# Other order tables for the last phase of a fused attention: its back half, the routing beside it, and the products of a constant

## The reference, cut to what matters

```python
G = jnp.cumsum(g, axis=-1)
logits = S * scale + (G[..., :, None] - G[..., None, :])
logits = jnp.where(tri, logits, -1e+30)
P = jax.nn.softmax(logits, axis=-1)
o = jnp.einsum('bhij,bhjd->bhid', P, v)
...
topv, topi = jax.lax.top_k(logits, TOP_K)
w = jax.nn.softmax(topv, axis=-1)
hidden = jax.nn.gelu(jnp.einsum('bld,efd->blef', x, w1) + b1, approximate=False)
```

## Time and profile before

| | |
|---|---|
| median of 3 runs | 2206.35 us (2200.0 to 2207.12) |
| the profiled execution: its own time, its span | 2211.93 us, 2210.1 us |
| busy over the span: TensorE, VectorE, ScalarE, GpSimd | 1998.4, 1590.3, 860.3, 763.0 us |
| mean granted clock of TensorE | 0.929 |
| the last attention phase | 1386.86 to about 1560 us |

### The profile page before, as it was taken

The page is one execution under the profiler, slowest core; times in us unless marked ns, Lnnn a source line. Parts: engine busy times, 40 slices in busy tenths (PEclk is TensorE's granted clock), DMA queues, the critical chain, the costliest instruction groups (busy, mean ns, idle before and its releaser), DMA issues. The chain is left out here.

```text
span 2210.1 us, 43938 instructions
## 1 busy us (share of the span) xinstructions
PE 1998.4 (90%) x16519; PEld 1336.5 (60%) x16519; DVE 1590.3 (72%) x3657; ACT 860.3 (39%) x1686; POOL 763.0 (35%) x823
## 2 busy tenths in 40 slices
PE   4898998898898999899889889989899999699996
PEld 2573564565465456356456546765799999445543
DVE  6969759948948966975994894541366766799996
ACT  2022233224134133223323423313156665498893
POOL 2523512641551451353254155040256665100000
PEclk7998999999899889899999989988899999899998
DMA  3000000000000000000000000030622222301000
GB/s 115 11 1 16 1 2 16 4 20 16 1 21 12 6 21 2 15 9 15 16 3 20 16 1 22 8 136 1 241 69 72 72 71 64 97 20 44 5 11 19
DMA packets 70177, 72.46 MB, mean 33 GB/s; under 512 B 12976, under 2 KB 58592, under 8 KB 69840
## 3 DMA queue, kind: packets, MB, share of 16 engines
q1 hardware_dynamic: 61296, 51.75, 7.8%
q0 software_dynamic: 8672, 17.91, 2.3%
HBM read 38.05 MB, written 27.43 MB: 30 GB/s over the span
## 5 line engine op out<-in xcount | busy, mean ns | idle before, releaser
L669 ACT ACTIVATE a_prep<-ps 128x1536 f32<-128x1536 f32 (+1 forms) x112 | 155.5, 1389 | 329.8 <-PE ps L1304 216.0
L897 DVE TENSOR_REDUCE a_mpart<-ps 128x4 f32<-128x512 f32 (+1 forms) x320 | 190.6, 654 | 51.8 <-PE ps L1245 36.3
L1839 ACT ACTIVATE b_hid<-ps,b_stage 128x128 f32<-128x128 f32 x572 | 163.0, 367 | 138.9 <-PE ps L1954 138.9
L1824 POOL DMA_INDIRECT rows_y<-b_orow,b_target x143 | 164.0, 1147 | 119.1 <-DVE b_orow L1929 116.3
L482 POOL TENSOR_TENSOR a_X<-a_X,a_txy 128x480 f32<-128x480 f32 (+14 forms) x240 | 180.9, 771 | 60.2 <-DVE a_txy L847 58.8
L476 POOL TENSOR_TENSOR a_K<-a_K,a_yU 128x480 f32<-128x480 f32 (+14 forms) x120 | 83.6, 697 | 311.6 <-DVE a_yU L842 310.5
L1117 PE MATMUL ps<-a_txy,cst 128*128 128x480 f32 (+14 forms) x480 | 177.6, 476 | 11.1 <-DVE a_txy L829 10.4
L1954 PE MATMUL ps<-b_hTp,b_stage 128*128 128x128 f32 x1144 | 152.8, 277 | 0.0
L1963 PE MATMUL ps<-b_stage,b_hid 128*128 128x128 f32 x1144 | 151.4, 275 | 0.3 <-ACT b_hid L1839 0.3
L864 DVE TENSOR_TENSOR a_mats<-ps,cst 128x512 f32<-128x512 f32 x112 | 69.9, 683 | 112.4 <-PE ps L1146 112.4
L1954 PEld LDWEIGHTS ps<-b_hTp,b_stage 128*128 128x128 f32 x1144 | 140.7, 194 | 0.0
(11 more groups left out here) (462 smaller groups left out, 4359.2 us busy)
## 6 DMA issues: line engine op xcount, KB each, us to landing
b_hrow<-rows_h SPq DMA_DIRECT2D x143, 65.0 KB, 1.8
b_w<-in_wexp SPq DMA_DIRECT2D x16, 514.0 KB, 10.1
d_got<-rows_y SPq DMA_DIRECT2D x32, 256.0 KB, 3.8
rows_h<-a_txy SPq DMA_DIRECT2D x19, 325.0 KB, 2.9
rows_y<-b_orow,b_target POOLq DMA_INDIRECT x143, 2.4
out<-xs SPq DMA_DIRECT2D x8, 256.0 KB, 2.3
cst<-in_const SPq DMA_DIRECT2D x1, 1865.5 KB, 14.5
rows_h<-a_mats,r_slot POOLq DMA_INDIRECT x112
```

The lines of the kernel that those rows point to most:

```text
L669: nc.scalar.activation(Pt[:, at:at + width, :], ps[:, 4:4 + width, :], ACT.Exp).then_inc(e_exp.sem, width)
L897: nc.vector.tensor_reduce(mpart[:, i, j, 4 * g:4 * g + 4], ps[:, 4 + n % 4, :].rearrange("p (r j) -> p r j", r=4)[:, :, 0:128 if i != j el ...
L1824: nc.gpsimd.indirect_dma_start(yrows, bass.IndirectOffsetOnAxis(target[:, p % DEEP:p % DEEP + 1], 0), orow[:, p % DEEP, :], None).then_inc ...
L1839: last = nc.scalar.activation(hid[:, p % 2, f, :], ps[:, p % 2, 128 * f:128 * f + 128], ACT.Gelu, bias=stage[:, p % 3, AT_B1 + f:AT_B1 + f ...
```

## The change

Four strings of `ORDER_END` are replaced. Of b, r and w each engine's string keeps as many as before (VectorE's has one r fewer; `weave` emits what is left over at the end). No instruction is added or taken away. The 175 products of the constant stay 175. Where instructions stand now:

| stretch of the last phase on TensorE | products of the constant before | after the change |
|---|---|---|
| L1154 to the first L1240 (A) | 13 | 23 |
| first L1240 to L1258 (B, the ten rounds) | 82 | 65 |
| L1258 to the first L1295 (C) | 33 | 36 |
| from the first L1295 to the last L1331 | 33 | 29 |
| from there to L1356, and behind L1356 | 14, 0 | 14, 8 |

```diff
 ORDER_END = {
-    'pe': ('bwwwwbbbbbbbbbbbbwbbbbbbbbwbbbbbbbbbbbbbwwwbbwwwwbbbbbbwwbwwbwwbwbbrwwwbwwbwwbrwwbrbwwwwwwbwwbwwbwwb'
...
+    'pe': ('bwwbwbbwbbbbbbbbbbwbbwbbbwwbbbbbbbbbbwwwbbbbwwwwwbwwwwbbwwwbbbbbwbwwwwwwwwrwbbwbbrwwbwwwwbbwbbbrbbwb'
...
-    'act': ('bbbbbbbbbbbbbbbbbbbbbbrrrrrrrbrbbbbbbbbbbbbbbbbbb'),
-    'po': ('bbbbrbbbrrrrrrrrrrbrrrrbrbrbbbbbb'),
+    'act': ('bbbbbbbbbbbbbrbbbbbbbrrrrrbbrrbbbbbbbbbbbbbbbbbbb'),
+    'po': ('bbbbbrbbbbbbbrbrbbrrrrrbrrrrrrrrr'),
 }
```

More of the change, by code:

```diff
@@ L183 @@
 ORDER_END = {
-    'pe': ('bwwwwbbbbbbbbbbbbwbbbbbbbbwbbbbbbbbbbbbbwwwbbwwwwbbbbbbwwbwwbwwbwbbrwwwbwwbwwbrwwbrbwwwwwwbwwbwwbwwb'
[L185 to L189, removed]
-    'act': ('bbbbbbbbbbbbbbbbbbbbbbrrrrrrrbrbbbbbbbbbbbbbbbbbb'),
-    'po': ('bbbbrbbbrrrrrrrrrrbrrrrbrbrbbbbbb'),
+    'pe': ('bwwbwbbwbbbbbbbbbbwbbwbbbwwbbbbbbbbbbwwwbbbbwwwwwbwwwwbbwwwbbbbbwbwwwwwwwwrwbbwbbrwwbwwwwbbwbbbrbbwb'
+           'bwwwwbwwwrbbwbbbwwwwbwwbbbbbwwwwrwbbbbrwwbwwbbbwwwwwbwbbbbbbwwwwwwwbbbwwwwwwwwwwbwwwwwwwbwwwwbwbwwbb'
+           'bwbbwwwwwbbbwwbbwbwwwbbwwbwbbwwwwwwwbbbbbwwwwwwwwbbbbbbbbwbbbbwwwwwbbbwbbbwbbbbbbbbbbbwwbbbbbbwbbbbw'
+           'bbbbbbwbbbbbwbbbwbbbbbbbbbbbwbbbbbbbwbbwbwbbbbbbbbbbbbbwbbwbbbbbbwwwwwwwwwbwwwwwbwwwwwwww'),
+    've': ('bbbbbbbrrbbbbbrbbbbbbbbbbbbrrrrrrrbrbbbrrrrbbbbrrrrbbbbrbbbbbbbbbbbbrrbbbbbbbbrbrbbbrbbbrbbbbbbbbbbb'
+           'bbbbbbbbbbrbbbbbbbbbbbbbb'),
+    'act': ('bbbbbbbbbbbbbrbbbbbbbrrrrrbbrrbbbbbbbbbbbbbbbbbbb'),
+    'po': ('bbbbbrbbbbbbbrbrbbrrrrrbrrrrrrrrr'),
 }
```

## The result

The changed kernel takes 2187.57 us (median of 5 runs, 2182.37 to 2192.13), the kernel before, run again beside it, 2207.12 (5 runs, 2200.0 to 2215.6). The ratio is 0.9906, 95% interval 0.9886 to 0.9926: 19.5 us or 0.94% faster. The forecast was 2189.5, the range 2180 to 2199. The profiled execution took 2190.87 us (span 2189.0, mean granted clock 0.935) against 2211.93 (2210.1, 0.929).

A forecast was written before the change was run, and what follows sets the result against it. Constant products standing in front of real work, and a low clock, were taken to bound the last attention phase. A +0.8, B -16.8, C -2.4, D -0.5 sum to -18.9 us, taken as -17 from the median: 2189.5, range 2180 to 2199.

The forecast's parts named there:

- A: Rotated keys and queries, start of the last attention phase: ten more constant products, partly filling a wait; net +0.8 us.
- B: Ten rounds of row maxima: fewer constant products, mostly in blocks under VectorE's maxima; -16.8 us including one low-clock stretch.
- C: Distances, L1258 to the first scores: seven products instead of 23 ahead of L1264, -5.2, later additions; net -2.4 us.
- D: Scores and values, end of the phase: 29 products among groups instead of 33, no fewer low-clock stretches; -0.5 us.
- signs of being wrong: Rounds over 5 us at full clock, over 40 us at 0.50, TensorE waiting behind POOL, or SP's writes ending after L1356.
- the walk of the new order at full clock: Rounds of row maxima: bare rounds 39.2 us plus 4.8 where blocks and routing don't fit under the maxima, 44.0.
- The one fall: Rounds of row maxima: one low-clock stretch of some 6 us after a sparse stretch, costing +2 us (0 to +6.5).
- Rival 2: More low clock in D and B: +6 and +3 us, leaving a gain of 8 to 10, 2197 us; chance 0.14.
- The other queues: POOL's scatters moved behind the third L509, SP's writes over the free rows ending 25 us before L1356: both cost nothing.
- Rival 1: Full clock throughout, no fall in B or D: -25.5 us, 2181 us; chance 0.14.
- Rival 3: Gain mostly one execution's: old B some 6.5 us shorter in most runs, one more new fall, -5 remains, 2201; chance 0.07.
- Rival 4: Slower: sparse order keeps the last phase at 0.50, losing 0.4 us per us; 100 us low gives 2221; chance 0.02.

The follow-up runs named there:

- changed kernel again: The changed kernel with no difference, run once more on another set's chip: 2187.65 us, ratio 0.9906 to the kernel before.
- three under each exp: The changed kernel with three constant products ahead of the first scores of each group waiting for an exp, 17 more in all: 2182.51 us, ratio 0.9866.

## Why the prediction was right, and where it was not

**The total** was right within 2 us, partly by luck. In the profiles the phase became 17.1 us shorter where the sum had 18.9: D was missed by 5.8, and B (3.2), C (0.5) and A (0.3) came out better by 4.0 in all. The two profiled executions differ by 21.1 since the second starts the phase 4.8 earlier; over all profiles here this start lies between 1378.57 and 1390.09, so it is no part of the gain. Of the signs of being wrong none came: the clock was at 0.50 for some 31 us of the phase, and the writes ended before L1356.

**A**: +0.8 predicted, +0.5 measured.

**B**, the walk of the new order at full clock: 44.0 against 41.28 (changed kernel again). Its parts: a bare round takes 3.70, not 3.8 (0.6 over six rounds), and the extras of rounds 0 to 3, 5, 6 and 8 came to 1.0, 0.25, 0.2, 0.55, 0.3, 0 and 0.3, 2.6 instead of 4.8. The mechanism was right, the extras were sized nearly twice too large. The one fall was placed and priced well: it came at round 3, after the sparse stretch of L1729 and L1730, lasted 3.5 instead of 6 us and cost 1.6 (42.86 - 41.28) instead of 2; but it is not in every execution. The old B's share is borne out by the same TensorE order at clock 0.99: 54.31. So of the 19.96 some 13.0 are place (54.31 - 41.28) and the rest, 8.5 less the new fall's 1.6, mostly the low clock of one execution. I had 12.3 and 6.5. VectorE's moved pieces may have a part in the 8.5: the kernel before and the one with fewer products ahead of L1264 (62.82 at 0.86, 71.20 at 0.73) give 0.40 us lost per us at 0.50 and 55.8 for the old B at full clock, an estimate. "The routing pieces on VectorE lie where it waits for TensorE anyway" holds for VectorE only: with the routing in its old places B is 50.32, not 41 to 43. So the full gain needs both: the products' new places without the routing's give half, the routing's without the products' nothing. With the old places TensorE waited 1.52 for ScalarE's L1586, and L1720 and L1744 stood between the third and the fourth L1240 of a round. What fraction of those 7.5 us or more is the clock (10 us low) is open; at 0.40 us per us it would be 4, an estimate.

**C**: L1264 1.9 behind L1258, measured 1.89; C -2.4, measured -2.95. The -5.2 is right for the profiled execution, whose block ran partly at 0.50; at full clock the step is worth 3.57 in the profile.

**D**: -0.5 predicted, +5.33 and +3.9 measured in the two profiles of the changed kernel. **This is the step that failed**: "The count per group falls to one from the fourth group on, though, so I see no reason for fewer low stretches than the 13.4 us here". I took the low time of one execution over as if it belonged to the order. By the granted clock (twice the missing clock times the length) it was 13.5 us before, 26.7 and 20.9 in the two profiles; over all profiles it lies between 3.5 and 26.7 with the changed places of the products and between 7 and 20 with the old ones. So the term should have been a range of some 8 us, not a number, and whether the fewer products make it worse stays open. At full clock the sum, 56.4, was met: 56.49 with three under each exp. Rival 2 has the size for D (+6) in these two profiles, not its second fall in B.

**The other queues**: nothing was paid, as costed. The scatters end 17.8 us behind the first scores (17 predicted); the writes were issued from 1481.26, 8 us earlier than predicted, mostly the earlier start and the shorter B. But "cost nothing" hid a condition: with the shares by place (L1689) as late as they are now, the old place of the scatters costs 23 us.

**Rival 1** (full clock throughout, 2181) is what three products under each exp nearly gave: 2182.51. **Rival 3** doesn't add up: 17 less 6.5 for the old B and less 3 for one more fall leaves 7.5, not 5. **Rival 4** (slower) rested on 0.4 us per us of low clock. That price holds for the old B, and in D of the changed order too: 10.3 us over 56.49 for 26.7 us low, 8.9 for 20.9. In rounds without products it is 0.2, and a phase without them with 113 us at 0.50 was still 8 us faster than before. The break-even of 63 us of low clock is refuted for that order; with the products no run had so much.

**The rule weighed.** In the changed kernel TensorE was busy 12.04 of the 12.63 us before the long fall, with no gap above 0.41 us, and fell; in B it was busy for all of the 12.6 us before the fall. In part B of the kernel without products it was busy 44.44 of 49.70 us and stayed at 0.50. The Trainium skill (TensorE: Matmul & The Clock Gate, HAM oscillation) describes falls that follow waits for transfers. The falls here don't follow such waits, so setting the rule aside for D was right. Full clock, which it gave for D, was reached in one profile of the two with three products under each exp; whether by the products themselves or by the gaps that they close is not shown.

## What to carry to other kernels

Filler meant to keep TensorE's clock up is free directly behind the last work that the other engine waits for; the same filler between the gates of the next round cost this kernel 21 us, place and clock together. A stretch in which TensorE is busy 98% of the time can still lose its clock. When a queue's inputs are moved later, move what waits for them behind the work that others need, and before explaining a difference of a few us, profile one kernel twice: the low clock of one execution is no property of the order.

## What the runs showed of the hardware

- Executions of one order differ in when and how long the clock is at 1.2 GHz: part B of the old order took 62.82 and 71.20 us, the new one 41.28 and 42.86.
- The clock can fall with no idle time ahead: TensorE was busy for all of the 12.6 us before the fall in B of the changed kernel, and for all of the 26.3 us at 0.50 in D.
- A round that is a chain over TensorE and VectorE loses 0.20 us per us at 1.2 GHz (4.65 against 3.70), since VectorE's 2.48 us don't change.
- VectorE's L948 takes 1.43 us for 128 columns and 1.42 for 96 where it starts while a scatter is being issued on GpSimd. With GpSimd's order of before, where no scatter is near, the same two take 0.28 and 0.25. Timeline, DVE, after:

```profile
1463.47 1.43 DVE L948 TENSOR_TENSOR a_prep<-a_prep 128x128 f32<-128x128 f32 x1
...
1465.51 1.42 DVE L948 TENSOR_TENSOR a_prep<-a_prep 128x96 f32<-128x96 f32 x1
```

The same, with GpSimd's order of before:

```profile
1497.03 0.28 DVE L948 TENSOR_TENSOR a_prep<-a_prep 128x128 f32<-128x128 f32 x1
...
1498.42 0.25 DVE L948 TENSOR_TENSOR a_prep<-a_prep 128x96 f32<-128x96 f32 x1
```

The scatters at 1462.51 and 1464.91 overlap or touch the two long ones, and an L509 follows each; the long ones end 0.16 and 0.13 us behind that L509. The Trainium skill (GPSIMD Engine Reference, Specifications) names contention between GpSimd and VectorE instructions with two SBUF inputs, which L948 has; the rows agree, and leave open whether the scatter or the L509 behind it is what L948 waits for.
